# Final norm and residual sum folded into the last turns of the layer pipeline, in place

## The reference, cut to what matters

```python
x = x + _layernorm(attn(_layernorm(x)))          # gives what the kernel calls x2
x = x + _layernorm(ffn(_layernorm(x)))           # ffn: 6 layers of local attention and gated MLP
return x
```

## Time and profile before

| | us |
|---|---|
| median of 3 runs | 4061.28 (4060.32 to 4062.5) |
| profiled execution, its own time | 4056.24 |
| its span | 4054.1 |
| from the end of the last write of X (DVE L1259) to the end of the span | 31.8 |

### The profile page before, as it was taken

How to read it: one execution, slowest core, us unless ns; L and a number is a source line. 1 busy time by engine, 2 the same in 40 slices (tenths; PEclk the granted TensorE clock), 3 DMA queues, 4 the chain that set the end, 5 groups by cost and what they waited for, 6 DMA issues and landing times. The chain is left out here.

```text
span 4054.1 us, 122291 instructions
## 1 busy us (share of the span) xinstructions
PE 3889.5 (96%) x43124; PEld 2846.0 (70%) x43124; DVE 3474.4 (86%) x8234; ACT 3728.1 (92%) x7250; POOL 2329.7 (57%) x2687
## 2 busy tenths in 40 slices
PE   4999999987999999999999999999999999999995
PEld 2555555554777777777777777777777777777774
DVE  4888888867888888888888888888888888888884
ACT  4889888867999999999999999999999999999995
POOL 4000000017777777777777777777777777777773
PEclk7999999998999999999999999999999999999997
DMA  6777778741111111111111111111111111111111
GB/s 186 249 243 236 246 241 250 239 149 45 40 45 44 49 45 40 45 45 49 45 40 45 45 49 45 40 45 45 50 45 40 45 45 50 44 40 45 45 50 54
DMA packets 249789, 348.35 MB, mean 86 GB/s; under 512 B 45105, under 2 KB 206365, under 8 KB 249117
## 3 DMA queue, kind: packets, MB, share of 16 engines
q1 hardware_dynamic: 249244, 340.94, 28.1%
HBM read 151.07 MB, written 82.85 MB: 58 GB/s over the span
## 5 line engine op out<-in xcount | busy, mean ns | idle before, releaser
L1490 PE MATMUL la_ps<-la_Wqkv,la_xsT 128*128 128x512 f32 x2304 | 1174.4, 603 | 6.1 <-DVE X L1186 6.1
L1186 DVE TENSOR_TENSOR X<-la_ps,la_tab 128x1024 f32<-128x1024 f32 x768 | 938.1, 1221 | 104.3 <-ACT la_sq L1334 97.3
L1116 POOL TENSOR_TENSOR la_rt<-X 128x512 f32<-128x512 f32 x384 | 495.1, 1289 | 586.9 <-PE la_ps L1505 436.8
L1133 POOL TENSOR_TENSOR la_rt<-la_rt,la_rn 128x1024 f32<-128x1024 f32 x384 | 722.9, 1904 | 29.9 <-POOL la_rn L1128 3.5
L1195 DVE TENSOR_REDUCE la_ssum<-la_sq 128x8 f32<-128x512 f32 x768 | 510.8, 665 | 0.0
L1334 ACT ACTIVATE la_sq<-la_ps 128x512 f32<-128x512 f32 x768 | 465.4, 606 | 35.6 <-PE la_ps L1490 30.9
L1117 POOL TENSOR_TENSOR la_rt<-X 128x512 f32<-128x512 f32 x384 | 494.8, 1289 | 0.0
L1521 PEld LDWEIGHTS la_ps<-la_kT,la_qB 128*64 128x64 f32 x12288 | 390.4, 138 | 85.1 <-issue 73.7
L1490 PEld LDWEIGHTS la_ps<-la_Wqkv,la_xsT 128*128 128x128 f32 x2304 | 362.8, 191 | 119.7 <-issue 75.4
L532 POOL COPY at_vh<-V 128x64 f32 (+1 forms) x64 | 15.3, 243 | 746.7 <-PE at_ps L743 746.6
L1521 PE MATMUL la_ps<-la_kT,la_qB 128*64 128x64 f32 x12288 | 432.9, 224 | 0.0
(11 more groups left out here) (205 smaller groups left out, 8871.6 us busy)
## 6 DMA issues: line engine op xcount, KB each, us to landing
at_band<-skew_scratch SPq DMA_DIRECT2D x64, 1536.0 KB, 7.4
la_vs<-la_v SPq DMA_DIRECT2D x192, 384.0 KB, 3.5
skew_scratch<-at_R SPq DMA_DIRECT2D x64, 1024.0 KB, 9.6
la_vs<-la_v SPq DMA_DIRECT2D x192, 128.0 KB, 3.4
la_Wqkv<-in_wqkv SPq DMA_DIRECT2D x28, 384.0 KB, 3.8
at_qh<-qt_scratch SPq DMA_DIRECT2D x64, 144.0 KB
at_kh<-kt_scratch SPq DMA_DIRECT2D x64, 144.0 KB
la_W<-in_L_ffn_W SPq DMA_DIRECT2D x24, 341.0 KB, 3.0
```

What stands on the lines that cost most here:

```text
L1116: e.tensor_tensor(dst[:, :, 0, :], c[:, :, 0, :], s[:, :, 1, :], ALU.add)
L1133: e.tensor_tensor(heads(rt, w), heads(rt, w), wide(rn[:, w * H:(w + 1) * H], D), ALU.mult)\
L1186: e.tensor_tensor(dst.rearrange("p f (h d) -> p f h d", d=D), ps[:, c % 2, :].rearrange("p (h d) -> p h d", d=D).unsqueeze(1).to_broadcast ...
L1490: e.matmul(ps[:, c % 2, :], xsT[:, m * P:(m + 1) * P], Wqkv[:, ds(layer(n) % 2, 1), c * 512:(c + 1) * 512], start=True, stop=True)\
```

## The change

`last_output()` is removed with its block. Its work is done inside `layers()`, in 9 pieces: seven of 4 tiles (k = 0 to 6, tiles 0 to 27) and two of 2 tiles (k = 7 and 8).

- SP: `x2_back(0)` and `x2_back(1)`, four loads of x2 each (256 KB a load), stand in turns 191 and 192 behind `v_shifted` and ahead of `y_shifted`. Both wait for POOL's `added(191, 1)`. The results go out after the last turn, piece by piece, straight from X.
- DVE: statistics and `mr` of the pieces 0 to 3 and `mr` of 0 to 2 between `mean_over(190)` and `with_x(191)` (statistics 4 and `mr` 3 stand behind `next_x(189)`); `mr` 4, statistics 5, 6, `mr` 5, statistics 7, `mr` 6 between `mean_over(191)` and `gated(191, 0)`; `mr` 7 behind `gated(191, 1)`; statistics 8, sum 7, `mr` 8 and sum 8 behind `next_x(191)`.
- POOL: roots 0 to 4 behind `with_b2(189)`, roots 5 to 7 behind `root(191)` and ahead of `with_b2(190)`, the sums of the pieces 0 to 6 behind the last turn, and then root 8.
- ACT: the norm is written over X itself (`out_one`): pieces 0 to 3 behind `y_turned(190)`, 4 behind `gelu(191, 0)`, 5 behind `gelu(191, 1)`, 6 to 8 behind the last turn.

Core of the diff:

```diff
+OUTS = [(k, k + G) for k in range(0, NT - G, G)] + [(NT - G, NT - G // 2), (NT - G // 2, NT)]
+ADDED_BY_POOL = NT // G - 1
...
-        layers(nc, a, X, X2, ident, x2_d)
-        last_output(nc, X, X2, x2_d, out)
+        layers(nc, a, X, X2, ident, x2_d, out)
...
+        def x2_added(e, k):
+            e.wait_ge(on_ev.sem, on_ev.v(k))
+            (to, hi) = OUTS[k]
+            for half in range(2 if hi > NT // 2 else 1):
+                e.wait_ge(x2_in[half], 16 * (NT // G // 2))
+            return e.tensor_tensor(x_final(k), X2[:, to:hi, :], x_final(k), ALU.add)
...   (SP)
+            def x2_back(half):
+                e.wait_ge(ad_ev.sem, ad_ev.v(TILES - 1, 2))
+                for k in range(half * NT // G // 2, (half + 1) * NT // G // 2):
+                    e.dma_start(X2[:, k * G:(k + 1) * G, :], x2_d[:, k * G:(k + 1) * G, :]).then_inc(x2_in[half], 16)
...
                 for n, m in t.back(0):
                     v_shifted(n, m)
+                if t.g in (TILES - 1, TILES):
+                    x2_back(t.g - TILES + 1)
                 for n, m in t.back(2):
                     y_shifted(n, m)
             straight(e, body, TILES, TB, DEEPEST)
+            for k, (to, hi) in enumerate(OUTS):
+                if k < ADDED_BY_POOL:
+                    e.wait_ge(by_pool.sem, by_pool.v(k))
+                else:
+                    e.wait_ge(by_dve.sem, by_dve.v(k - ADDED_BY_POOL))
+                e.dma_start(rows_out[:, to:hi, :], x_final(k)).then_inc(sent, 16)
...   (POOL; root(191) and with_b2(189) stand ahead of these)
+                if t.g == TILES + 5:
+                    for k in range(5, 8):
+                        los[k].root(e, k)
                 for n, m in t.back(7):
                     with_b2(n, m)
+                if t.g == TILES + 4:
+                    for k in range(5):
+                        los[k].root(e, k)
             straight(e, body, TILES, TB, DEEPEST)
+            for k in range(ADDED_BY_POOL):
+                x2_added(e, k).then_inc(by_pool.sem, 1)
+            los[8].root(e, 8)
...   (DVE, behind mean_over)
+                if t.g == TILES + 3:
+                    out_stats(0); out_stats(1); out_mean(0); out_stats(2); out_mean(1); out_stats(3); out_mean(2)
+                if t.g == TILES + 4:
+                    out_mean(4); out_stats(5); out_stats(6); out_mean(5); out_stats(7); out_mean(6)
...   (DVE, behind next_x)
+                if t.g == TILES + 3:
+                    out_stats(4); out_mean(3)
+                if t.g == TILES + 5:
+                    out_stats(8)
+                    x2_added(e, 7).then_inc(by_dve.sem, 1)
+                    out_mean(8)
+                    x2_added(e, 8).then_inc(by_dve.sem, 1)
...   (ACT)
+            def out_one(k):
+                (to, hi) = OUTS[k]
+                e.wait_ge(mr_ev.sem, mr_ev.v(k))
+                for j, x in enumerate(range(to, hi)):
+                    act = e.activation(X[:, slot(x), :], X[:, slot(x), :], ACT.Identity, bias=mr[:, x, :],
+                                       scale=los[k].st[:, j, 8:9])
+                act.then_inc(on_ev.sem, 1)
```

More of the change, by code:

```diff
@@ L134, in root @@
         e.wait_ge(self.stats.sem, self.stats.v(step))
-        e.tensor_tensor(self.st[:, :, 8:9], self.st[:, :, 7:8], self.power[:], ALU.pow)\
+        e.tensor_tensor(self.st[:, :, 8:9], self.st[:, :, 7:8], self.power[:, 0:self.n, :], ALU.pow)\
             .then_inc(self.rstd.sem, 1)
@@ L937, in _, with layers @@
                 casts(e)
-def layers(nc, a, X, X2, ident, x2_d):
+def layers(nc, a, X, X2, ident, x2_d, out):
     with Part(nc, "la") as t:
@@ L988, in layers @@
         ln = Norm(t, "ln", 1)
+        mr = t.sb("mr", [P, NT, 1])
+        x2_in = [t.sem(f"x2{half}") for half in range(2)]
+        mr_ev, on_ev = t.mark("mre"), t.mark("one")
+        by_pool, by_dve, sent = t.mark("adp"), t.mark("add"), t.sem("sent")
+        lo = Norm(t, "lo0", G)
+        los = [lo] + [Norm(t, f"lo{k}", hi - to, lo) for k, (to, hi) in enumerate(OUTS) if k]
+        rows_out = out.rearrange("b (t p) d -> p (b t) d", p=P)
         BANK_S, BANK_F, BANK_Y = 2, 6, 7
@@ L1100, in _ @@
             ln.open(e)
+            lo.open(e)
             e.wait_ge(s_set, SET)
@@ L1260, in next_x, with out_stats, out_mean @@
                                 yb[:, (m - 1) % 4:(m - 1) % 4 + 2, :], ALU.add).then_inc(x_ev.sem, 1)
+            def out_stats(k):
+                (to, hi) = OUTS[k]
+                if k == 6:
+                    e.wait_ge(x_ev.sem, x_ev.v(TILES // 2 - 3))
+                elif k > 6:
+                    e.wait_ge(x_ev.sem, x_ev.v(TILES // 2 - 9 + k))
+                else:
+                    e.wait_ge(x_ev.sem, x_ev.v(TILES // 2 - 5))
+                los[k].take(e, [X[:, slot(x), :] for x in range(to, hi)], k)
+            def out_mean(k):
+                (to, hi) = OUTS[k]
+                e.wait_ge(lo.rstd.sem, lo.rstd.v(k))
+                e.scalar_tensor_tensor(mr[:, to:hi, :], los[k].st[:, :, 6:7], -1.0, los[k].st[:, :, 8:9],
+                                       ALU.mult, ALU.mult).then_inc(mr_ev.sem, 1)
             def body(t):
@@ L1268, in body @@
                     mean_over(n, m)
+                if t.g == TILES + 3:
+                    out_stats(0)
+                    out_stats(1)
+                    out_mean(0)
+                    out_stats(2)
+                    out_mean(1)
+                    out_stats(3)
+                    out_mean(2)
+                if t.g == TILES + 4:
+                    out_mean(4)
+                    out_stats(5)
+                    out_stats(6)
+                    out_mean(5)
+                    out_stats(7)
+                    out_mean(6)
                 for n, m in t.back(3):
@@ L1301, in body @@
                         gated(n, m, 1)
+                if t.g == TILES + 4:
+                    out_mean(7)
                 for n, m in t.back(0):
@@ L1307, in body @@
                         next_x(n, m)
+                if t.g == TILES + 3:
+                    out_stats(4)
+                    out_mean(3)
+                if t.g == TILES + 5:
[3 more added lines that the diff above has]
+                    x2_added(e, 8).then_inc(by_dve.sem, 1)
                 for n, m in t.back(5):
@@ L1443, in body @@
                     y_turned(n, m)
+                if t.g == TILES + 4:
+                    for k in range(4):
+                        out_one(k)
                 for n, m in t.back(2):
@@ L1453, in body @@
                         gelu(n, m, 0)
+                if t.g == TILES + 5:
+                    out_one(4)
                 for n, m in t.back(3):
@@ L1461, in body @@
                         gelu(n, m, 1)
+                if t.g == TILES + 5:
+                    out_one(5)
                 for n, m in t.back(1):
@@ L1466, in _ @@
             straight(e, body, TILES, TB, DEEPEST)
+            for k in range(6, len(OUTS)):
+                out_one(k)
         @block.tensor
@@ L1673, in _ @@
             straight(e, body, TILES, TB, DEEPEST)
[L1676 to L1742, removed]
```

4 lines of the change are left out of this document (added).

## The result

| | before | changed |
|---|---|---|
| median | 4060.8 us (6 runs, 4057.22 to 4064.9) | 4036.4 us (6 runs, 4031.87 to 4039.08) |
| ratio of the times | | 0.9939, 95% interval 0.9929 to 0.9949 |
| profiled execution: its span | 4054.1 | 4033.9 |

The account below looks back on a forecast made before the run. TensorE bounds the long middle; the end is a serial 31.8 us stage waiting for all of X. -25.6 + 0.8 - 0.25 + 0.15 = -24.9 takes the median from 4061.28 to 4036.4 us; range 4034 to 4039, with rivals to 4041, low end 4031.

Parts of the forecast that it names:

- the tail: Behind the last write of X: 6.2 us left for the last piece instead of 31.8, so 25.6 saved; bounds 5.6 and 7.5.
- the queue: x2 loads ahead of Y's shift of tile 189: `stats(189)` about 1 us late, 0.8 after slack, bounds 0 and 4.0.
- `mean_over`: On DVE, `mean_over(191)` no longer held by POOL's `with_b2(190)`, since roots 5 to 7 come between: 0.25 us gained.
- the hole ahead of `gated`: DVE's 4.29 us of idleness ahead of `gated(191, 0)`: the work put there costs 0.15 us, bound 0.9.
- the large term: The serial last stage of 31.8 us leaves, its work done in idle time of the last turns: 25.6 us saved.
- Table loads: Rival: on ACT, pieces 4 and 5 each need table loads around them, 3.0 us more, 4039.4; chance 0.03.
- the bound of 0.9: DVE ahead of `gated(191, 0)`: cost up to 0.9 us if `mr` 6 is caught behind POOL's root 7.
- One sign of being wrong: At the end of the kernel, results that leave more than 1.5 us apart would show the prediction wrong.
- The queue at its full 4 us: Rival: Y's shift of tile 189 waits for all of `x2_back(0)`, 4.0 us instead of 0.8, 4039.6; chance 0.12.
- The lock: Rival: DVE and POOL instructions around pieces 6 to 8 catch each other, 2.5 us in all, 4038.9; chance 0.10.
- unchanged pace: Rival: at the end the pieces still leave 3.28 us apart, only 10 us saved; chance 0.02 for no change.
- slower than before: Rival: the 1 MB ahead of Y's shift delays `stats(189)` by more than 34 us; chance 0.02.

Follow-up runs that it names:

- experiment 9: Changed kernel with the x2 loads behind Y's shift and all nine pieces behind the last turn; median 4049.67 us, ratio 0.9978 to the kernel before.
- experiment 7: Changed kernel with the x2 loads behind Y's shift and DVE's sum 7 behind `mr` 8; root 8 took 0.70 us, not 0.85.
- experiment 8: Changed kernel with the x2 loads behind Y's shift and statistics 4 and `mr` 3 ahead of `with_x(191)`, which came at 27.61 us instead of 26.47.
- experiment 6: Changed kernel with POOL's roots 5 to 7 behind `with_b2(190)`; `mean_over(191)` took 0.40 us again.
- the second trace: Changed kernel run once more, unedited; from SP's first issue of `v_shifted(191)` to the end of the span 53.32 us, against 54.81 in its first trace.

## Why the prediction was right, point by point

**Total.** 4036.4 was forecast and 4036.4 measured. That they agree to the tenth is luck: from the anchor 24.9 us were forecast, and 23.6 and 25.1 (78.39 - 53.32) found in two traces. In the first of them the tail gave 26.1 (25.6 forecast), the queue cost 1.33 (0.8), `mean_over` gave 0.25 (0.25), the hole ahead of `gated` cost 0 (0.15), and 1.4 came from a term that the sum doesn't have. The mechanism of the large term, the stage's work done in the holes, is shown by experiment 9.

**What is left at the end.** 6.2 forecast, 5.71. The steps: statistics from the end of `next_x` at 4028.19 to 4029.21, 1.02 (0.88); root 8 until 4030.14, 0.93 (1.0), held by 0.15 as experiment 7 shows; `mr` 8 until 4030.33, 0.19 (0.2); the activations until 4031.24, 0.91 (0.9); sum 8 until 4031.70, 0.46 (0.45); the transfer until 4033.9, 2.2 (2.8). The size that was most off is the transfer: counting the halved bytes at nothing was wrong by 0.6. From issue to landing the 256 KB results take 2.3 us and the two of 128 KB 1.8.

**The holes.** DVE ahead of `with_x(191)`: 0 forecast, 0 found, with 0.35 to spare (experiment 8). Ahead of `gated(191, 0)`: 0.15 forecast, 0 found. ACT and POOL: 0, as forecast; POOL idled 0.72 ahead of sum 6. Table loads: none. The Trainium skill, "ScalarE: Activation LUTs", section "Table sets: the hidden batching unit", says that identity is in every set; the trace agrees (activations of pieces 4 and 5 at 4017.89 and 4021.05 without a load).

**The hold of `mean_over(191)`.** 0.25 forecast, 0.24 found, and given back in experiment 6. The Trainium skill, "SBUF — State Buffer", section "SBUF: two separate sides", says that whichever of the two engines starts first keeps the shared port pair to its end. POOL's sum agrees: DVE is held by it (0.40 against 0.16). POOL's root does not agree in full. Root 8 lost 0.15 us (0.85 against 0.70) of the 0.28 for which DVE's sum 7, started first, ran beside it. The other way round, root 7 (4017.69 to 4018.39) had started first and `mr` 6, with two SBUF operands, took 0.17 at 4017.75 all the same. So the bound of 0.9, for `mr` 6 caught behind root 7, was not a risk here.

**The queue.** The place and the sign were right, the delay low: about 1 us, less 0.2 of slack, was forecast; 1.5 to 1.6, less 0.25, came. I had looked for it in the landing of the shift, behind issues of unchanged length. It lies in the issue: the second one for Y grew from 0.87 to 2.29, and what follows its end took 2.12 instead of 2.05.

**The missing step.** I forecast that a delay at `stats(189)` passes on "whole". It can grow: TensorE runs partly empty behind it, and in one trace its granted clock fell to 0.50 for about 3 us and added 1.4. The prediction has no row of the clock for this stretch, and did not ask whether it could fall there. It is in no term and no bound of the prediction; 0 in one execution and 1.4 in another, so it doesn't change the verdict here.

**The signs.** Several of the signs that I had named are narrowly missed. The end of `next_x(191)` came at 4028.19; less the 3.38 us by which the anchor is later, that is 4024.81, with 4021.5 to 4024.5 forecast (4023.29 in the second trace, inside). The end of the span came 5.7 behind it, not 6 to 7; `stats(189)` was 1.58 and 1.49 late, with 1.5 as the limit; DVE idled 0.25 ahead of `with_x(191)`, where none was forecast. One sign of being wrong even came: the last two results leave 2.13 us apart (issues at 4029.60 and 4031.73), over 1.5. It was badly chosen, since the prediction's own steps (root 8, `mr` 8, two activations, sum 8, less sum 7) already put them 2.1 apart.

**The rivals.** The queue at its full 4 us needs more than four loads ahead (eight made it 5.6). The lock costs 0.15 us in the tail, because the work in the holes seldom meets POOL's sums; in experiment 9, where the same work is packed behind the last turn, it holds the epsilon step for over 0.8 us five times. The prediction called that step free by the rows of the last stage; rows of an earlier stage of the same trace (912.08, above) showed it held. Table loads and unchanged pace are out by the rows above, and slower than before by the times.

## What to carry to other kernels

A last stage that starts only when everything is done can be laid into the idle time of the turns ahead of it, piece by piece, if each engine's hole is added up beforehand: four statistics of some 1.4 us fitted into 6.1 us, and a fifth came out at the end for all but 0.35 us. Put loads for that stage behind the small transfers on which the chain waits: here the same loads lengthened D1 by 1.2 us ahead of one, by 2.7 where the clock fell as well, and by nothing behind it. Where two engines exclude each other, the order of the instructions is worth something: 0.24 us for `mean_over(191)` and 0.15 for root 8 here. And a single trace can carry 1.4 us that the next one of the same kernel does not have; take a second one before explaining a difference of that size.

## What the runs showed of the hardware

- An SP issue stretches with what is queued: the second issue for Y takes 0.87 us with none or two loads of 256 KB ahead, 1.12 with three, 2.29 (2.24 in a second trace) with four and 4.44 with eight. What stands behind on SP waits too. In three traces the second issue of `v_shifted(191)` took 1.11 to 1.18 instead of 0.60 with no x2 load ahead of it, so something else can stretch an issue as well.
- The lower level of TensorE's clock fell in different places in executions with the same work ahead of it: on `out_proj(190)` in one trace (2.59 us), on `out_proj(191)` in one whose only other difference is the order of POOL's roots (3.48 us), on neither in a third.
- A DVE instruction with a single SBUF operand can be held by POOL too: the epsilon step on 2 or 4 elements a partition takes 0.17 free and 1.03 to 1.17 beside POOL's sum in experiment 9, and 1.58 beside a memset of POOL in the kernel before. Beside POOL's root it took 0.17, and so did `mr` 6 in the changed kernel (two SBUF operands of 4 elements). The step on a single element took at most 0.156 in the 192 instructions of the layers, but none of these met any work of POOL, so whether it would be held stays open.
- POOL's power on one, two and four elements a partition takes 0.55, 0.70 and 1.02 us.
- The scatter of the times of this kernel, some 8 to 10 us, lies almost wholly ahead of the last turns and of the layers: the anchor and the first issue of Y's shift moved together, by 11 us over the 13 traces, while D2 repeated within 0.08 over the eight that share the end of the changed kernel.
